# Mamba layer: work moved off VectorE to ScalarE and TensorE, and the products du*B of four states in sixteen made by GpSimd

## The reference

```
u, z = split(x @ in_w.T);  u = silu(conv4(u) + conv_b)
dt = softplus(x_dbl[:, :DT_RANK] @ dt_w.T + dt_b);  B, C = the other 32 rows of x_dbl = u @ xproj_w.T
dA = exp(dt * A);  dBu = dt * B * u           # A is -exp(A_log), one number per channel and state
h = dA_t * h + dBu_t;  y_t = sum over the 16 states of h * C_t
y = (y + u * D) * silu(z);  out = y @ out_w.T
```

## Time and profile before

| what | value |
|---|---|
| median of 3 runs | 2815.53 us (2811.09 to 2817.47) |
| profiled execution | 2811.5 us, its span 2809.7 us |
| Mamba stage: first to last scan | starts at 72.4 and 1123.6 us |
| busy share of the span | PE 85%, DVE 76%, ACT 52%, POOL 42% |
| DMA | 8 GB/s mean, idle in the Mamba stage |

### The profile page before, as it was taken

The page is one execution under the profiler, slowest core; times in us unless marked ns, Lnnn a source line. Parts: engine busy times, 40 slices in busy tenths (PEclk is TensorE's granted clock), DMA queues, the critical chain, the costliest instruction groups (busy, mean ns, idle before and its releaser), DMA issues. The chain is left out here.

```text
span 2809.7 us, 46598 instructions
## 1 busy us (share of the span) xinstructions
PE 2401.2 (85%) x14880; PEld 1568.5 (56%) x14880; DVE 2138.4 (76%) x3085; ACT 1455.2 (52%) x2617; POOL 1191.9 (42%) x864
## 2 busy tenths in 40 slices
PE   2778878778887877799779999699999989978997
PEld 0233333333333332577578888466666767767776
DVE  3899999999999999577555555588888867764555
ACT  2666666666666774466332222466666646642010
POOL 4566667666666667333300000455555533231000
PEclk9899999999999999899789999899999999988999
DMA  2000000000000000200000000000000010000000
GB/s 84 1 0 0 1 0 1 1 1 0 0 0 0 0 1 0 63 12 12 22 1 1 1 0 0 6 0 0 0 0 0 1 48 11 11 4 1 11 7 12
DMA packets 35414, 22.17 MB, mean 8 GB/s; under 512 B 22710, under 2 KB 34017, under 8 KB 34801
## 3 DMA queue, kind: packets, MB, share of 16 engines
q1 hardware_dynamic: 35312, 20.98, 2.9%
HBM read 18.87 MB, written 2.10 MB: 7 GB/s over the span
## 5 line engine op out<-in xcount | busy, mean ns | idle before, releaser
L784 POOL TENSOR_TENSOR m_hc<-m_h,m_cs 128x1024 f32<-128x1024 f32 x256 | 603.2, 2359 | 351.9 <-DVE m_h L706 344.6
L706 DVE TENSOR_TENSOR_SCAN m_h<-m_da,m_pdb 128x1024 f32<-128x1024 f32 x256 | 585.1, 2286 | 23.5 <-DVE m_pdb L661 5.0
L456 PE MATMUL m_py<-m_hc,ident 128*128 128x512 f32 x1024 | 514.6, 627 | 4.2 <-DVE m_y L670 2.1
L579 ACT ACTIVATE m_da<-m_dt,m_aneg 128x508 f32<-128x508 f32 x512 | 337.8, 709 | 47.8 <-POOL m_dt L753 46.1
L661 DVE TENSOR_TENSOR m_pdb<-m_du,m_pdb 128x1024 f32<-128x1024 f32 x256 | 314.8, 1230 | 42.7 <-POOL m_du L760 11.4
L456 PEld LDWEIGHTS m_py<-m_hc,ident 128*128 128x128 f32 x1024 | 202.2, 200 | 213.6 <-issue 174.6
L594 ACT ACTIVATE m_cs<-m_pc 128x512 f32<-128x512 f32 x256 | 150.5, 588 | 219.7 <-PE m_pc L446 219.6
L442 PE MATMUL m_pdb<-m_bcrow,m_sel 96*128 96x512 bf16 x256 | 101.8, 397 | 171.8 <-DVE m_h L706 170.8
L1391 ACT ACTIVATE c_act_of<-c_pg 128x512 f32<-128x512 f32 x144 | 86.2, 598 | 237.3 <-PE c_pg L212 237.3
L1759 POOL TENSOR_TENSOR d_pr<-d_pr,d_rden 128x512 f32<-128x512 f32 x128 | 133.3, 1041 | 177.2 <-DVE d_rden L1690 177.2
L1037 ACT ACTIVATE x_prT<-x_pt 77x512 f32<-77x512 f32 x256 | 137.8, 587 | 130.6 <-PE x_pt L939 129.5
(11 more groups left out here) (257 smaller groups left out, 5373.7 us busy)
## 6 DMA issues: line engine op xcount, KB each, us to landing
cw_gu<-in_C_gu SPq DMA_DIRECT2D x1, 2304.0 KB
x<-in_x SPq DMA_DIRECT2D x8, 256.0 KB, 4.9
fw_w<-in_F_w SPq DMA_DIRECT2D x1, 2048.0 KB
out_x<-x SPq DMA_DIRECT2D x8, 256.0 KB, 2.3
bm_mrow<-in_B_mrow SPq DMA_DIRECT2D x1, 1232.0 KB, 6.5
x_ctxT<-in_B_ctxT SPq DMA_DIRECT2D x32, 38.5 KB, 1.8
x_mask<-in_B_mrow SPq DMA_DIRECT2D x32, 38.5 KB, 2.8
x_ctxT<-in_E_ctxT SPq DMA_DIRECT2D x32, 38.5 KB, 1.8
```

Of the source, the lines that this page charges most:

```text
L456: ins = mm(py[:, c, :], S.ident[:, :], hc[n % BUF][:, place(n, c), :], start=n == 0, stop=n == NS - 1)
L579: A_(dst, src, ACT.Exp, scale=aneg[:, d, c, n:n + 1]).then_inc(s["da_ready"], 1)
L706: V.tensor_tensor_scan(h[n % BUF][:, way], da[n % BUF][:, d:d + CH * GT][:, way], pdb[:, b:b + 2, :].rearrange("p c t -> p (c t)")[:, way] ...
L784: P.tensor_tensor(hc[n % BUF][:, :, :], h[n % BUF][:, :].rearrange("p (c t) -> p c t", c=CH), bc(cs[n % BUF][:, :], 1, CH), ALU.mult).then ...
```

## The change

Four things are done.

1. `norm` goes from DVE to ACT: eight activations (Identity with a bias and a scale of one number per partition) take the place of eight tensor_scalar. POOL prepares two more small arrays of constants (`nmean`, `mr12`) once.
2. u*D is added by PE: two matmuls of a diagonal matrix `skip` with `us`, as the first of a unit's accumulation in `py`. `sum_up` is then two copies from `py` to `y1` by ACT.
3. L650 becomes a scalar_tensor_tensor with a factor of 1.0; its inputs stay the same.
4. For the states n = 4, 7, 10 and 13 (`APART`) DVE makes no product. PE spreads B_n into `pc` four steps ahead, between two rows of C; ACT copies it to the new SBUF tile `bs`; POOL, two steps ahead, multiplies du by `bs` into the new SBUF tile `db`; DVE's scan reads `da` and `db`, both in SBUF.

```
+    APART = (4, 7, 10, 13)
+    NA = len(APART)
+        bs = A.sb("bs", [128, GT])
+        db = A.sb("db", [128, CH * GT])
...
@@ PE, spread(u, n, d)
+                    if n not in APART:
+                        if due(N - 1):
+                            pe.wait_ge(s["h_ready"], N - 1)
+                        mm(pdb[:, row_bank(n), :], sel[:, n, :], bcrow[d][:, :],
+                           start=True, stop=True).then_inc(s["b_mm"], 1)
                     if due(N):
                         pe.wait_ge(s["c_ready"], N)
+                    if n - 1 + 3 in APART:
+                        pe.wait_ge(s["bs_ready"], apart(u, n + 2) + 1)
                     mm(pc[:, :], sel[:, NS + n, :], bcrow[d][:, :],
                        start=True, stop=True).then_inc(s["c_mm"], 1)
+                def spread_apart(u, n, d):
+                    pe.wait_ge(s["c_ready"], NS * u + n - 2)
+                    mm(pc[:, :], sel[:, n, :], bcrow[d][:, :], start=True, stop=True).then_inc(s["bs_mm"], 1)
...
@@ PE, add_state, at n == 0
+                        for c in range(CH):
+                            mm(py[:, c, :], skip[:, d, c, :], us[d][:, c, :], start=True, stop=False)
@@ PE, end of a step
+                        if n + 4 in APART:
+                            spread_apart(u, n + 4, d)
@@ ACT
+                def norm(g):
...
+                        ins = A_(xh[:, i:i + 1, :], S.x[:, b, :], ACT.Identity, bias=mr12[:, b], scale=r12[:, b])
...
+                        ins = A_(S.x[:, b, :], S.x[:, b, :], ACT.Identity, bias=mr1[:, b], scale=r1p[:, b])
+                def sum_up(u, d):
+                    act.wait_ge(s["y_mm"], NS * (u + 1))
+                    if due(u):
+                        act.wait_ge(s["ys_ready"], u)
+                    for c in range(CH):
+                        A_(y1[:, c, :], py[:, c, :], ACT.Copy).then_inc(s["y1_ready"], 1)
...
+                        if n + 3 in APART:
+                            act.wait_ge(s["bs_mm"], apart(u, n + 3) + 1)
+                            if due(apart(u, n + 3)):
+                                act.wait_ge(s["apart_ready"], apart(u, n + 3))
+                            A_(bs[:, :], pc[:, :], ACT.Copy).then_inc(s["bs_ready"], 1)
+                        if n == 3 and not (isinstance(u, int) and u == 0):
+                            sum_up(u - 1, 1 - d)
@@ DVE
-                        V.tensor_tensor(bcrow[d][64:96, :], rest[64:96, :], bcrow[d][64:96, :],
-                                        ALU.subtract).then_inc(s["row_ready"], 1)
+                        V.scalar_tensor_tensor(bcrow[d][64:96, :], rest[64:96, :], 1.0, bcrow[d][64:96, :],
+                                               ALU.mult, ALU.subtract).then_inc(s["row_ready"], 1)
...
+                        if n in APART:
+                            dve.wait_ge(s["apart_ready"], apart(u, n) + 1)
+                        else:
+                            dve.wait_ge(s["db_ready"], beside(u, n) + 1)
...
+                        add = db[:, :] if n in APART else pdb[:, b:b + 2, :].rearrange("p c t -> p (c t)")
                         V.tensor_tensor_scan(h[n % BUF][:, way], da[n % BUF][:, d:d + CH * GT][:, way],
+                                             add[:, way], 0.0, ALU.mult, ALU.add).then_inc(s["h_ready"], 1)
                         if n + 1 < NS:
+                            if n + 1 not in APART:
+                                step(u, n + 1, d)
@@ POOL, ahead of step n's own product
+                        if n + 2 in APART:
+                            k, i = apart(u, n + 2), APART.index(n + 2)
+                            pool.wait_ge(s["bs_ready"], k + 1)
+                            pool.wait_ge(s["du_ready"], u + 1)
+                            if due(k):
+                                last = NS * u + APART[i - 1] if i else NS * (u - 1) + APART[-1]
+                                pool.wait_ge(s["h_ready"], last + 1)
+                            way = slice(None, None, 1 if (n + 2) % 2 == 0 else -1)
+                            P.tensor_tensor(db[:, :].rearrange("p (c t) -> p c t", c=CH), du[d][:, way, :],
+                                            bc(bs[:, :], 1, CH), ALU.mult).then_inc(s["apart_ready"], 1)
```

More of the change, by code:

```diff
@@ L305, in mamba_layer @@
         mr1 = A.sb("mr1", [128, NB])
+        nmean, mr12 = A.sb("nmean", [128, NB]), A.sb("mr12", [128, NB])
+        skip = A.sb("skip", [128, 2, CH, 128])
         xh = A.sb("xh", [128, GS, D])
@@ L342, in row_bank, with apart, beside @@
             return 2 * (n % 2)
+        def apart(u, n):
+            return NA * u + APART.index(n)
+        def beside(u, n):
+            return (NS - NA) * u + n - sum(k < n for k in APART)
         def place(n, c):
@@ L379, in _ @@
                 pe.wait_ge(s["prep"], 2)
+                pe.wait_ge(s["skip_ready"], 2 * CH)
                 def front(g, d, at=None):
@@ L508, in _ @@
                 act.wait_ge(s["seg_zero"], BUF + 1)
+                act.wait_ge(s["rstd"], STEPS)
                 par = [0]
+                def norm(g):
+                    if isinstance(g, int) and g == 1:
+                        act.wait_ge(s["rstd"], 2 * STEPS)
+                    if due(g):
+                        act.wait_ge(s["lnT_mm"], g)
+                    for i in range(GS):
+                        b = bass.ds(g * GS + i, 1)
+                        ins = A_(xh[:, i:i + 1, :], S.x[:, b, :], ACT.Identity, bias=mr12[:, b], scale=r12[:, b])
+                    ins.then_inc(s["xh_ready"], 1)
+                    act.wait_ge(s["xh_ready"], g + 1)
+                    for i in range(GS):
+                        b = bass.ds(g * GS + i, 1)
+                        ins = A_(S.x[:, b, :], S.x[:, b, :], ACT.Identity, bias=mr1[:, b], scale=r1p[:, b])
+                    ins.then_inc(s["xres_ready"], 1)
+                def sum_up(u, d):
[4 more added lines that the diff above has]
+                        A_(y1[:, c, :], py[:, c, :], ACT.Copy).then_inc(s["y1_ready"], 1)
                 def front(g, d, at=None):
                     u = 2 * g + d
+                    if at is None:
+                        norm(g)
                     if d == 0 and at in (None, 1):
@@ L525, in front @@
                             A_(zraw[:, c, :], pm[1 - c][:, :], ACT.Copy).then_inc(s["z_raw"], 1)
+                    if d == 1 and at == 5 and not (isinstance(g, int) and g + 1 == NG):
+                        norm(g + 1)
                     if at in (None, 6):
@@ L594, in scan @@
                         A_(cs[n % BUF][:, :], pc[:, :], ACT.Copy).then_inc(s["c_ready"], 1)
+                        if n + 3 in APART:
[5 more added lines that the diff above has]
+                            sum_up(u - 1, 1 - d)
                         if nxt:
                             nxt(n)
+                    if not nxt:
+                        sum_up(u, d)
                 drive(act, front, scan, par)
@@ L608, in _ @@
                 V.tensor_copy(sel[:, :, :], bc(W.sel32[:, :], 2, 128)).then_inc(s["prep"], 1)
+                for d in range(2):
+                    for c in range(CH):
+                        V.tensor_scalar(skip[:, d, c, :], S.ident[:, :], W.dskip[:, d, c:c + 1], None, ALU.mult
+                                        ).then_inc(s["skip_ready"], 1)
                 dve.wait_ge(s["aexp_ready"], 1)
@@ L611, in _ @@
                 find_batches_with_keys(nc, dve, masks)
-                dve.wait_ge(s["rstd"], STEPS)
                 par = [0]
-                def norm(g):
-                    if isinstance(g, int) and g == 1:
-                        dve.wait_ge(s["rstd"], 2 * STEPS)
-                    if due(g):
-                        dve.wait_ge(s["lnT_mm"], g)
-                    for i in range(GS):
-                        b = bass.ds(g * GS + i, 1)
-                        ins = V.tensor_scalar(xh[:, i:i + 1, :], S.x[:, b, :], S.mean[:, b],
-                                              r12[:, b], ALU.subtract, ALU.mult)
-                    ins.then_inc(s["xh_ready"], 1)
-                    dve.wait_ge(s["xh_ready"], g + 1)
-                    for i in range(GS):
-                        b = bass.ds(g * GS + i, 1)
-                        ins = V.tensor_scalar(S.x[:, b, :], S.x[:, b, :], r1p[:, b], mr1[:, b],
-                                              ALU.mult, ALU.subtract)
-                    ins.then_inc(s["xres_ready"], 1)
                 def front(g, d, at=None):
                     u = 2 * g + d
-                    if at is None:
-                        norm(g)
-                    if d == 1 and at == 5 and not (isinstance(g, int) and g + 1 == NG):
-                        norm(g + 1)
                     if at in (None, 9):
@@ L662, in step @@
                                     ALU.mult).then_inc(s["db_ready"], 1)
-                def sum_up(u, d):
-                    dve.wait_ge(s["y_mm"], NS * (u + 1))
-                    if due(u):
-                        dve.wait_ge(s["ys_ready"], u)
```

(4 more changed lines are left out.)

46 lines of the change are left out of this document (20 added, 26 removed).

## The result

The changed kernel takes 2869.8 us (median of four executions, 2867.9 to 2871.3) against 2813.5 for the kernel before (four executions; the 2815.5 ahead of the prediction is the median of three): ratio 1.0199, interval 1.0185 to 1.0214. The prediction was 2785 with a range up to 2832. The miss is 85 us, and the sign is wrong.

A forecast was written before the change was run, and what follows sets the result against it. DVE bounds the kernel before; after the change POOL with its port would, at 64.0 us per unit for 65.96: 31 us off over 16 units, 1.5 on, predicted 2785. Own range 2765 to 2812; 8 in 10, 2672 to 2832.

The forecast's parts named there:

- So the stage is DVE's own list: Mamba stage before the change: DVE alone sets the pace, 65.96 us per unit, with hardly any waits for PE or POOL.
- Exclusion: DVE instructions with two SBUF inputs and POOL products shut each other out, including the four scans; chance 0.42.
- walk: One unit stepped through under exclusion from scan 0: 63.2 us, POOL with its port the bound, held or busy 62.3.
- the gain of 0: L650 as scalar_tensor_tensor: possible gain 0 to 0.9 us per unit, taken as 0.
- L650 is the only one that stretches: Among DVE's lines only L650, with two SBUF inputs, lengthens beside POOL: 0.68 us in the head, else 1.61.
- All of this lies beside DVE: Work added per unit to ACT (5 us) and PE (2 us) is covered by their waits of 13 and 10 us.
- late links: Allowance for waits that now show, such as dt for ACT's softplus: 0.8 us per unit, making 64.0.
- Prices of single items: Added work priced singly: ACT's norm 3.4 us every other unit, copies 0.588 each, PE's skip matmuls 1.88.
- both levels: PE's clock levels: four fp32 instructions take 1.88 us at the full clock, 3.52 at the lower.
- PE or ACT late: Rival without exclusion: PE's load or ACT's norm ahead of Silu delays rest, 60 us a unit, 2722; chance 0.10.
- the world without exclusion: Rival for the four scans: DVE at 56.0 and POOL at 53.1 run side by side, median 2682; chance 0.22.
- POOL keeps the port: Slower rival: POOL's next ready product goes before DVE's waiting `db` scan, 67.2 us per unit, median 2837; chance 0.14.

The follow-up runs named there:

- e3: Changed kernel, but the scans of states 4, 7, 10 and 13 read old contents of PSUM instead of `db`, POOL's products kept: 2843.9 us.
- e4: Changed kernel, but POOL's product `db` covers 8 of 512 columns per chunk, the rest staying zero: 2854.9 us.
- e10: Changed kernel with two of the four convolution taps left out, less PE work: 2842.6 us.
- e18: Changed kernel with Identity and Copy in place of the two Silu forms, so no table loads there: 2809.9 us.
- e13: Changed kernel with the norm moved from n = 5 to n = 1 of the unit: 2858.8 us.
- e1: Changed kernel with `APART` empty: norm, sum_up, skip and new L650 stay, DVE makes all products: 2822.3 us, ratio 1.0036.
- e8: Kernel before with only the norm moved to ACT and L650 in its new form: 2798.2 us, ratio 0.9945.
- e22: Changed kernel with the row of C of state 7 copied by ACT between the two Silus: 2859.2 us.
- e21: Kernel before with norm on ACT at n = 1, L650's new form, and state 7's row of C copied between the two Silus: 2781.5 us.

## Why the prediction was wrong

- **What bounds the kernel.** "So the stage is DVE's own list" was true as an average, and for the rest of each unit and the units with the norm. From scan 3 to scan 9 of the unit without a norm PE is busy 22.5 of 24.0 us, no less than DVE. I never took the busy time by window over that stretch; its nearest sign in my rows, L678 standing 5.6 us for PE, was read as nothing.
- **Exclusion: right for the scans, too narrow as a rule.** The hc of POOL that starts 0.16 us after the scan takes 4.24 us instead of 2.36 and ends at 509.02, 2.13 behind the scan's end at 506.89. In sum POOL's 256 hc are held (2857 - 2359) ns x 256 = 127 us, 8.0 a unit; my walk had 4 x 2.29 = 9.2. DVE's scans pay (2498 - 2286) ns x 64 = 14 us, by their mean of 2498. L697 at 1.33, and 0.68 in the head, shows that its new form is held too, so the gain of 0 was right. What exclusion costs the kernel is 26 us (e3). The Trainium skill's rule of one read port that the later one waits for ("SBUF — State Buffer", section "Who interferes with whom") agrees with the scans and with L697. But "L650 is the only one that stretches" misread the rows: of the four L623 of a norm the first starts 0.25 us behind a product `hc` and takes 2.2 us in six of seven cases, its followers 0.33, and the earlier trace rows shows it as a mean of 712 ns against 344 for L629. It reads one tensor, not two, and writes to SBUF. Nothing in the sum hangs on it, since the norm leaves DVE. The rows of the means, then L623 in the kernel before:

```profile
L836 POOL TENSOR_TENSOR m_hc<-m_h,m_cs 128x1024 f32<-128x1024 f32 x256 | 728.3, 2857 | 129.4 <-DVE m_h L746 99.7 <-PE m_py L482 25.3 <-ACT m_cs L651 2.1
L746 DVE TENSOR_TENSOR_SCAN m_h<-m_da,m_db 128x1024 f32<-128x1024 f32 x64 | 159.9, 2498 | 5.7 <-ACT m_da L636 3.5 <-POOL m_db L828 1.8 <-POOL m_hc L836 0.2
...
L623 DVE TENSOR_SCALAR m_xh<-x,mean,m_r x32: 330/336/2203, 37.9 to 891.9; 128x128 f32<-128x128 f32 x16, 128x128 f32 x16
```

- **The walk: right outside the stretch,** 38.3 against 38.1, and in its parts: scan 9 to 13 14.3 against 13.5 and 13.6, scan 13 to the next scan 3 24.0 against 24.6 and 24.5. There POOL and its port do decide: without them it falls on to 36.6 (e3) and 37.6 (e4). From scan 3 to scan 7 its 16.1 against 15.4 was luck: in e3, without the port, these steps are the same to 0.01 us, and two taps less on PE shorten them (e10).
- **The failed step:** "All of this lies beside DVE: ACT's and PE's waits of 205 and 158 us over the stage, 13 and 10 us per unit, cover their 5 and 2 us", with 0.8 us for late links. Of PE's 13 idle us a unit (40 of 200 us in the earlier trace rows) only 4.2 and 1.5 lie in the stretch (28.37 - 24.17 and 24.02 - 22.50). In it PE and ACT release each other in turn: PE's next row waits for ACT's copy of the last, ACT's copy stands behind norm and Silu, and DVE's product behind both. Into this loop the change puts 1.7 us of skip on PE, `bs` rows and copies (PE's waits there are new: 35.0 us ahead of them and 18.3 behind), and 3.3 us of norm on ACT right ahead of the block of 5 us. The stretch takes 30.8 us on average for 24.9: 5.9 x 16 = 94 us, less the 13 I had put in for late links, makes 81 of the 85 us missed. Shown by removal are the Silu block (60 us, e18), PE's load (27, e10), the port (26, e3), POOL's load (15, e4) and the norm's place (11, e13); these overlap. That the `bs` hand-overs themselves are a cost is argued by elimination only, as the stretch stays at 33.2 / 30.6 without the port and at 32.3 / 29.9 without POOL's load, against 28.5 / 27.0 in e1; no run takes the hand-overs out.
- **Prices of single items: right.** Norm in ACT 1.65 us for four, 3.3 in all (predicted 3.4); `bs` 0.597 (0.588); the skip matmuls 1.88 to the pipeline's end. I priced each item well and hid it under cover that isn't where the item stands.
- **A multiplier left out.** PE can work slower after it has stood: the x projection at 524.14 takes 2.96 us for 1.88. It takes 2.8 to 3.6 us in 11 of 16 units of the changed kernel, 14 us in all above 1.88, and 1.88 (once 1.97) in every unit of the kernel before. I knew both levels and took them as given, not as something that the change moves.
- **Rivals.** "PE or ACT late" named the cause, with the place (norm ahead of Silu, rest at n = 9), but only in the world without exclusion, at 60 us a unit, and with a chance of 0.10. I priced no case in which exclusion and late rows hold at once; that is the one that came. "POOL keeps the port" didn't come: most of the `db` scans (36 of 64) went on time, with a median of 2279 ns.

Not settled: how e1's loss over e8 (25 us) divides between PE's skip and ACT's y1, what the `bs` hand-overs cost, and e22 above. Removing single costs doesn't give a sum; that each also moves the clock of PE's next matmuls is one reason.

## What to carry to other kernels

An average of an engine's slack is no cover: before work is laid on a second engine, take the busy times by window over the stretch in which that work will stand, and list what waits for what there. Where two engines hand single-buffered rows (one buffer, refilled only once it is read) to each other, look for blocks of one of them (here two table loads and a norm) that hold up the other's rows. Placing the hand-over inside the block is a cheap repair to try: it gave 12 us in e21 and 11 in e22. Of a bundle of moves each is worth timing by itself: here the norm's was a gain of 15 us, inside a bundle that lost 56.
